# A decoder kernel on one core: the bf16 parts of the ternary stage shared out anew, and small moves in the state-space stage

## What is computed

```
u     = silu(conv4(in_proj @ context))
B, C  = x_proj @ u                    # 16 rows each
delta = softplus(dt_proj @ dt_lo + b)
s_t   = s_(t-1) * exp(delta_t * A) + (delta_t * u_t) * B_t
y_t   = sum_n s_t * C_t
x     = x + (y + D * u) * silu(norm(x))
```

```
xn        = norm(x)
gate, up  = split(xn @ ternary(w_gate_up).T)     # 1024 columns each
h         = silu(gate) * up
x         = x + rms_norm(h) @ ternary(w_proj).T
```

## Time and profile before

| | |
|---|---|
| median of three runs | 2121.33 us (2117.27 to 2121.64) |
| the profiled execution | 2119.57 us, its span 2117.3 us |
| state space, from its first VectorE memset to the last addition to x | 135.09 to 290.80 us |
| ternary, from its first ScalarE instruction | 290.89 us on |
| its main loop's first and its unit 4's first matmul | 308.39 and 321.92 us |
| TensorE, VectorE, ScalarE, GpSimd busy | 88%, 57%, 39%, 12% |

### The profile page before, as it was taken

The page is one execution under the profiler, slowest core; times in us unless marked ns, Lnnn a source line. Parts: engine busy times, 40 slices in busy tenths (PEclk is TensorE's granted clock), DMA queues, the critical chain, the costliest instruction groups (busy, mean ns, idle before and its releaser), DMA issues.

```text
span 2117.3 us, 26070 instructions
## 1 busy us (share of the span) xinstructions
PE 1871.3 (88%) x9285; PEld 1218.1 (58%) x9290; DVE 1203.8 (57%) x2828; ACT 831.1 (39%) x1972; POOL 250.5 (12%) x239
## 2 busy tenths in 40 slices
PE   7898969887595999999899689999997999997798
PEld 3554535655453566666565465555554777777455
DVE  7639988365744455555587773333335666665222
ACT  4348954023521333333446123333332555553111
POOL 5210000011023100000110200000001222220111
PEclk9897989898797999999999899999999999998899
DMA  3010000002443000000100312000002000003110
GB/s 144 1 60 0 1 21 1 30 2 90 196 174 124 0 1 1 1 1 1 40 1 2 160 45 95 1 1 0 1 1 122 1 1 1 1 1 139 51 34 14
DMA packets 17391, 82.53 MB, mean 39 GB/s; under 512 B 3152, under 2 KB 10068, under 8 KB 13040
## 3 DMA queue, kind: packets, MB, share of 16 engines
q1 hardware_dynamic: 11184, 70.70, 8.5%
q0 software_dynamic: 2944, 8.03, 1.3%
q10 hardware_dynamic: 3136, 2.13, 0.3%
HBM read 72.57 MB, written 8.81 MB: 38 GB/s over the span
## 4 chain that ended last, share of the span: by engine, by line
PE 75%; DVE 16%; issue 3%; ACT 3%; POOL 1%; DMA 1%; POOLq 0%; another core or an unknown queue 0%; DVEq 0%; ACTq 0%; SPq 0%
PE bank L136 61%; PE bank L141 9%; PE bank L3798 4%; DVE space L985 3%; PE bank L3820 2%; DVE space L1594 1%; DVE space L3290 1%; DVE space L992 1%; DVE space L174 1%; DVE space L185 0%; POOL space L2872 0%; ACT space L1788 0%; DVE space L2636 0%; ACT space L1083 0%; POOLq L4312 0%
## 5 line engine op out<-in xcount | busy, mean ns | idle before, releaser
L136 PE MATMUL bank<-space 128*128 128x256 f32 (+15 forms) x6735 | 1435.4, 414 | 63.0 <-DVE space L2821 6.0
L136 PEld LDWEIGHTS bank<-space 128*128 128x128 f32 (+5 forms) x6740 | 882.0, 177 | 556.4 <-issue 371.9
L141 PE MATMUL bank<-consts,space 128*128 128x128 f32 (+1 forms) x1874 | 291.6, 298 | 151.7 <-DVE space L185 50.2
L141 PEld LDWEIGHTS bank<-consts,space 128*128 128x128 f32 (+1 forms) x1874 | 237.2, 153 | 230.1 <-issue 125.4
L2667 ACT ACTIVATE space<-bank,space 128x256 f32<-128x256 f32 x128 | 59.5, 470 | 95.7 <-DVE space L2621 95.7
L2872 POOL TENSOR_TENSOR space<-space,consts 128x4 f32<-128x4 f32 x64 | 68.6, 1071 | 218.2 <-DVE space L2803 218.2
L193 POOL TENSOR_TENSOR space<-space,consts 128x4 f32<-128x4 f32 x18 | 20.4, 1131 | 620.5 <-DVE space L180 620.5
L2621 DVE TENSOR_REDUCE space<-bank 128x2 f32<-128x512 f32 x64 | 44.0, 688 | 86.9 <-PE bank L136 86.8
L2525 ACT ACTIVATE space<-bank,space 128x128 f32<-128x128 f32 (+1 forms) x128 | 52.7, 416 | 84.5 <-DVE space L2492 84.5
L136 PE MATMUL bank<-space,consts 128*128 128x512 f32 (+2 forms) x148 | 75.7, 630 | 11.4 <-DVE space L992 9.1
L2795 DVE TENSOR_REDUCE space<-bank 128x2 f32<-128x512 f32 x64 | 44.2, 691 | 69.2 <-PE bank L136 69.1
(11 more groups left out here) (375 smaller groups left out, 1963.3 us busy)
## 6 DMA issues: line engine op xcount, KB each, us to landing
space<-in_L_ffn SPq DMA_DIRECT2D x13, 2048.0 KB, 11.8
space<-in_L_attn SPq DMA_DIRECT2D x9, 2048.0 KB, 11.7
space<-in_L_xattn SPq DMA_DIRECT2D x4, 2048.0 KB, 9.8
expert_results<-space SPq DMA_DIRECT2D x16, 128.0 KB
space<-expert_results SPq DMA_DIRECT2D x8, 256.0 KB, 4.6
space<-in_L_xattn SPq DMA_DIRECT2D x1, 1663.0 KB, 17.5
space<-in_L_xattn SPq DMA_DIRECT2D x1, 1536.0 KB, 6.7
space<-in_L_attn SPq DMA_DIRECT2D x1, 1344.0 KB, 14.1
```

The source lines that it names most:

```text
L136: return self.nc.tensor.matmul(out, lhsT, rhs, start=first, stop=last, skip_group_check=True)
L141: return self.nc.tensor.transpose(out, src, eye)
```

## The change

State space: VectorE's copy of B (`bT`) moves from ahead of the statistics to behind the second pair of delta and du. TensorE turns du's first half before it spreads C's second half; ScalarE copies that half of C after the first decay. The last unit's multiply by C goes by halves, and each of TensorE's last sums waits for its own half (`weighted` counts 33). The four multiply-adds with D go in the order of f, and each pair waits for its own f's sums.

Ternary: `Norm` is written out in the stage: VectorE makes the moments and a shift, GpSimd the roots, ScalarE normalises (`normalise`). For the first half of the tokens TensorE turns xn by ordinary f32 matmuls with the identity, ScalarE casts a part from the bank, and TensorE subtracts it from the bank by a matmul with minus identity (`take_away`); the low part is again a cast of the bank. The second half keeps VectorE's subtractions, later. VectorE copies the first quarter out. `UNITS` run over both f of a quarter for the first half of tokens, then for the second; units 0 and 1 need the first half alone, unit 2 waits for the second. ScalarE's Abs and Sign of the second quarter come after all parts.

```
 # StateSpace.tensor
         for g in range(NG):
             self.spread_half(e, 0, g)
-        for g in range(NG):
             e.wait_ge(*s.du_ready(2 * g + 2))
...
                 for g in range(NG):
+                    if u == N - 1 and g:
+                        e.wait_ge(*s.weighted.all)
 # StateSpace.vector
-        e.wait_ge(*s.bT_mm.all)
-        nc.vector.tensor_copy(flat(self.bT), bk[6][:, 0:NT * SSM_N]).then_inc(*s.bT_out.one)
...
+            if p == 1:
+                e.wait_ge(*s.bT_mm.all)
+                nc.vector.tensor_copy(flat(self.bT), bk[6][:, 0:NT * SSM_N]).then_inc(*s.bT_out.one)
...
-                nc.vector.tensor_tensor(y, y, self.cc[n % 3], ALU.mult).then_inc(*s.weighted.one)
-        e.wait_ge(*s.summed.all)
-        for p, (f, g) in enumerate(self.CUTS):
+                if t < N:
+                    nc.vector.tensor_tensor(y, y, self.cc[n % 3], ALU.mult).then_inc(*s.weighted.one)
+                else:
+                    for g in range(NG):
+                        nc.vector.tensor_tensor(y[:, cut(g)], y[:, cut(g)], self.cc[n % 3][:, cut(g)],
+                                                ALU.mult).then_inc(*s.weighted.one)
+        for f, g in ((0, 0), (0, 1), (1, 0), (1, 1)):
+            e.wait_ge(*s.summed(2 * SSM_N - 1 + f))
 # StateSpace.scalar
-        for g in range(NG):
-            self.c_half(e, 0, g)
+        self.c_half(e, 0, 0)
...
         self.decay(e, 0)
+        self.c_half(e, 0, 1)
         e.wait_ge(*s.du_by_vector.all)
         self.weigh_b(e, 0, 1)
 # Ternary
-    UNITS = [(f, g) for f in range(TERN_H // P) for g in range(NG)]
+    UNITS = [(2 * n + f, g) for n in range(TERN_H // (2 * P)) for g in range(NG) for f in range(2)]
 # Ternary.tensor
+        for i in range(4):
+            e.wait_ge(*s.normed(i + 1))
             for k in range(DC):
+                done = c.mm(bk[k][:, i * P:(i + 1) * P], self.xn[:, i, k * P:(k + 1) * P], c.ident, i == 0, i == 3)
...
+        self.take_away(e, self.parts[0], s.high, s.rest)
+        for i in range(4, NT):
+            e.wait_ge(*s.normed(i + 1))
+            for k in range(DC):
+                done = c.turn(bk[4 + k][:, i % 4 * P:(i % 4 + 1) * P], self.xn[:, i, k * P:(k + 1) * P])
...
         self.turn_quarter(e, 0)
+        self.take_away(e, self.parts[1], s.middle, s.last)
         e.wait_ge(*s.gu_out(1))
...
+            if u == 0:
+                e.wait_ge(*s.low.all)
+            if u == 2:
+                e.wait_ge(*s.low_by_vector.all)
...
+    def take_away(self, e, part, taken, left):
+        c, s = self.c, self.s
+        e.wait_ge(*s.minus.all)
+        for k in range(DC):
+            e.wait_ge(*taken(k + 1))
+            c.mm(c.banks[k], self.minus, part[:, k, 0:HALF], False).then_inc(*left.one)
 # Ternary.vector
-        self.norm.vector(e)
+        for g in range(NG):
+            self.moments(e, g)
         first = self.gate_up[0]
+        self.shifts(e, 0)
         first.limits(e)
+        self.shifts(e, 1)
         first.above(e)
         first.through(e)
+        e.wait_ge(*s.gu_turned(1))
+        nc.vector.tensor_copy(self.guT[0], bk[6].bitcast(BF16).rearrange("p (a b) -> p a b", b=HALF)).then_inc(*s.gu_out.one)
+        for k in range(DC):
+            e.wait_ge(*s.high(DC + k + 1))
+            nc.vector.tensor_tensor(self.rest[k], bk[4 + k], self.parts[0][:, k, HALF:TOK], ALU.subtract).then_inc(*s.kept.one)
+        for k in range(DC):
+            e.wait_ge(*s.middle(DC + k + 1))
+            nc.vector.tensor_tensor(self.parts[2][:, k, HALF:TOK], self.rest[k], self.parts[1][:, k, HALF:TOK],
+                                    ALU.subtract).then_inc(*s.low_by_vector.one)
...
-            e.wait_ge(*s.squared(15 + g))
+            e.wait_ge(*s.squared(14 + 2 * g))
 # Ternary.scalar
+        nc.scalar.activation(self.minus, c.ident_bf, ACT.Copy, scale=-1.0).then_inc(*s.minus.one)
         e.wait_ge(*self.ld.all)
         self.gate_up[0].scalar(e)
+        self.normalise(e, 0)
+        for k in range(DC):
+            e.wait_ge(*s.x_turned(k + 1))
+            nc.scalar.activation(self.parts[0][:, k, 0:HALF], bk[k], ACT.Copy).then_inc(*s.high.one)
+        self.normalise(e, 1)
...
+        for k in range(DC):
+            e.wait_ge(*s.kept(k + 1))
+            nc.scalar.activation(self.parts[1][:, k, HALF:TOK], self.rest[k], ACT.Copy).then_inc(*s.middle.one)
         self.gate_up[1].scalar(e)
...
+    def normalise(self, e, g):
+        c, s = self.c, self.s
+        e.wait_ge(*s.shift(g + 1))
+        for i in range(4 * g, 4 * g + 4):
+            c.nc.scalar.activation(self.xn[:, i, :], c.x[:, i, :], ACT.Identity, bias=self.rs[:, 2, i:i + 1],
+                                   scale=self.rs[:, 0, i:i + 1]).then_inc(*s.normed.one)
```

More of the change, by code:

```diff
@@ L1204, in __init__ @@
         self.s = c.signals(
-            x_turned=4, high=4, rest=4, middle=4, low=4, gu_turned=4, gu_out=4, p_turned=2, p_out=2, gate_mm=16,
+            var=2, inverse=2, shift=2, normed=NT, minus=1, x_turned=4, high=4, rest=2, kept=2, middle=4, last=2, low=2, low_by_vector=2, gu_turned=4, gu_out=4, p_turned=2, p_out=2, gate_mm=16,
             up_mm=16, silu=16, inner=16, squared=16, totals=2, sums=1, mean=1, scale=1, out_mm=NT, added=NT)
@@ L1219, in tensor @@
             cs = slice(g * HALF, (g + 1) * HALF)
-            if u < 2:
-                e.wait_ge(*s.low(2 * g + 2))
-            if f % 2 == 0 and g == 0 and f:
+            if u == 0:
+                e.wait_ge(*s.low.all)
+            if u == 2:
+                e.wait_ge(*s.low_by_vector.all)
+            if u % 4 == 0 and u:
                 e.wait_ge(*s.gu_out(f // 2 + 1))
@@ L1353, in scalar, with moments, shifts @@
                                  ACT.Copy).then_inc(*s.p_out.one)
+    def moments(self, e, g):
+        c, s, nc = self.c, self.s, self.c.nc
+        cs = slice(4 * g, 4 * g + 4)
+        for i in range(4 * g, 4 * g + 4):
+            nc.vector.bn_stats(self.stats[:, i, :], c.x[:, i, :]).then_inc(*c.v.next())
+        e.wait_ge(*c.v.so_far)
+        for i in range(4 * g, 4 * g + 4):
+            nc.vector.bn_aggr(self.mv[:, i, :], self.stats[:, i, :]).then_inc(*c.v.next())
+        e.wait_ge(*c.v.so_far)
+        nc.vector.tensor_scalar(self.rs[:, 1, cs], self.mv[:, cs, 1], 1.0, 1e-5, ALU.mult, ALU.add).then_inc(*s.var.one)
+    def shifts(self, e, g):
+        s, cs = self.s, slice(4 * g, 4 * g + 4)
+        e.wait_ge(*s.inverse(g + 1))
+        self.c.nc.vector.scalar_tensor_tensor(out=self.rs[:, 2, cs], in0=self.mv[:, cs, 0], scalar=-1.0,
+                                              in1=self.rs[:, 0, cs], op0=ALU.mult, op1=ALU.mult).then_inc(*s.shift.one)
+    def normalise(self, e, g):
+        c, s = self.c, self.s
+        e.wait_ge(*s.shift(g + 1))
+        for i in range(4 * g, 4 * g + 4):
+            c.nc.scalar.activation(self.xn[:, i, :], c.x[:, i, :], ACT.Identity, bias=self.rs[:, 2, i:i + 1],
+                                   scale=self.rs[:, 0, i:i + 1]).then_inc(*s.normed.one)
     def square(self, e, u):
@@ L1367, in gpsimd @@
         c, s = self.c, self.s
-        self.norm.gpsimd(e)
+        for g in range(NG):
+            cs = slice(4 * g, 4 * g + 4)
+            e.wait_ge(*s.var(g + 1))
+            c.nc.gpsimd.tensor_tensor(self.rs[:, 0, cs], self.rs[:, 1, cs], c.minus_half[:, 0:4],
+                                      ALU.pow).then_inc(*s.inverse.one)
         e.wait_ge(*s.mean.all)
```

47 lines of the change are left out of this document (17 added, 30 removed).

## The result

The changed kernel takes 2106.27 us (median of 6, 2105.89 to 2107.76), the kernel before on the same chip 2119.32 (median of 6, 2115.86 to 2126.2): ratio 0.9942, interval 0.9925 to 0.9959. Two later comparisons gave 0.9946 (0.9919 to 0.9973) and 0.9931 (0.99 to 0.9963).

A forecast was written before the change was run, and what follows sets the result against it. The chain of waits gave TensorE three quarters of the span and VectorE a sixth; the diff touches four hand-overs. Terms 3.35 + 1.3 + 2.9 = 7.55 us; 7.5 from 2120.5 gives 2113.0, range 2108.5 to 2118.5.

The forecast's parts named there:

- Start of the state space: VectorE's 4.03 us idle ahead of the statistics goes; second scan at 168.48, 3.35 us earlier, bounds 1.7 to 3.35.
- Rival (a): State-space clock rise stays in place, one or two ternary hand-overs are longer: gain 4.9 us, 2115.6; chance 0.22.
- End: End of the state space: two multiply-adds run under TensorE's last sum, gates 1.3 us earlier, bounds 1.0 and 1.38.
- Start of the ternary stage: Main loop 14.4 us after the stage's first ScalarE instruction instead of 17.50; 2.9 of the 3.1 us left at unit 4.
- the 2.4 us: Ternary main loop: what the low clock costs after its start, counted in when TensorE wants the second quarter (26.0).
- rival (c): TensorE's clock is high as the ternary main loop starts; unit 4 at 27.3, gain 3.7 us, total 2112.2; chance 0.15.
- The term for the stage: Ternary stage's share of the forecast gain: 2.9 us, with unit 4 at 28.1 against 31.03 before.
- my lower bound: Ternary start: VectorE's copy of the first quarter from PSUM takes between 0.69 and 1.2 us.
- the last low part: Ternary stage of the kernel before: the last of four lows ends just before 308.39, where TensorE's main loop begins.
- (b): The second quarter is the new wait in the ternary stage; unit 4 slips to 30 or 31, total 2117.5; chance 0.15.
- The tail: End of the ternary stage: later quarters, projection and tail keep their code; an earlier first total gains nothing.
- Rival (d): Slower: the clock in the state-space scans doesn't rise; 2125 us with 30 us more of low clock; chance 0.05.

The follow-up runs named there:

- before_warm: The kernel before, with 25 idle matmuls filling TensorE's two gaps ahead of the ternary main loop; ratio 0.9962 against the kernel before.
- early_both: The changed kernel with the second quarter's Abs, Sign and limits made earlier, in two idle holes; 0.9912 and 0.9906 against the kernel before, medians 2109.65 and 2108.5 us.

## Why the prediction was right, and where it was wrong

- **Start of the state space**: right in place and size (second scan forecast for 168.48, found at 168.50). Rival (a), that the rise of the clock stays where it is, didn't happen in the pair that was compared; as the rise varies by 6 us in the unchanged kernel, that it moved along is in part luck.
- **End**: right, 1.29 for 1.3, under the sum that was named.
- **Start of the ternary stage**: the chain was right, one term wrong. The step that failed is the 2.4 us that I let the low clock cost after the start of the main loop, copied from the trace of before. It measured 0: the change closes the gaps ahead of the loop, and so the loop starts high (42 matmuls in 9.22). That is rival (c), to which I gave 0.15. `before_warm` shows it by itself: the old code with the gaps filled has unit 4 2.96 us earlier. The term for the stage was 2.9 and measured 4.3 to 4.5. Rival (c) said 3.7 with unit 4 at 27.3, bound by the second quarter; it came at 26.49, bound by it. The 0.8 between is the same clock, which was high from 9.95 on: the second half's and the quarter's turning ended at 12.18 (forecast 12.6) and the second take-away took 0.64 us (0.9), so that ScalarE reached the quarter's Abs at 15.9 instead of 16.7, and it was ready at 24.3 instead of 25.3. VectorE's copy of the first quarter took 0.69, my lower bound, but held nothing up: it ended at 12.9, and the loop waited for ScalarE's low parts. The Trainium skill (VectorE: DVE Perf Modes, Why PSUM operands drop a tier) lets 16-bit operands in PSUM keep the two-fold mode, and the 0.69 for 1024 elements agrees: 512 in f32 took as long.
- **A reading that was wrong**: the last low part doesn't end before 308.39. VectorE's four run from 306.57 to 309.07, and unit 0 waits for the first two alone. The sum doesn't use it.
- **The second quarter** became the new wait, with 1.42 us, as rivals (b) and (c) have it, but on an earlier loop. `early_both` takes it away and gains 1.48.
- **The tail** was costed at nothing and isn't constant: the down projection's first 64 matmuls take 14.05, 15.6 to 15.7, or 17.1 us by the clock.
- **The rest of the kernel, and the range**: the two stages gave 9.0 where the sum has 7.55, and 9.0 off 2120.5 would be 2111.5, within the range. What put the time below it is the second failed step: the other ten stages stand in the sum at nothing. In the profiled pair they gave 4.6 us, in the timed comparisons 4 to 5.5, and their cause is open. The range was built from four executions of the kernel before, whose scatter I took for that of any pair. Stages that the diff doesn't touch differed by up to 17.7 us in sum between profiles (1852.9 to 1870.6 over all kernels). The two later medians of the changed kernel, 2112.66 and 2113.49, are on the forecast 2113.0 by luck: the kernel before took 2126 to 2128 beside them. And the range isn't pulled in, as it says: its own bounds are 2108.8 and 2117.9.
- **Rival (d)**, slower: no sign of it.

## What to carry to other kernels

Here a chain of casts and subtractions ahead of a long run of matmuls cost twice: by its length, and by the low clock that the run then started with. When a change fills TensorE's gaps ahead of such a run, price the first microseconds of the run at the high clock, and look next for the engine whose work comes late because the run now comes early. And for changes under a per cent, read the stage's length in several profiles: the time of the whole execution scattered by 20 us where the change was worth 9. Read the granted clock of the timed executions beside it.

## What the runs showed of the hardware

Stages with the same instructions take one of a few lengths (two contexts: 148.9 to 159.2), by how much low clock falls into them. Whole executions of one kernel take 0.37 to 0.41 us more for each microsecond more at 1.2 GHz. The clock rose behind 3.4 to 3.7 us of transposes alone in five of eight profiles, and in three it didn't. A plain f32 matmul of 128 columns is two instructions; eight such matmuls took 3.75 us at the low clock, where eight transposes took 2.07.
